# A shorter schedule for the convolution stages of a four-part image kernel: stages one step closer, one signal split in two

## The reference

```python
t = t + dwconv(t, cpe1_w, cpe1_b)                 # depthwise 3x3, "cpe1"
tn = layernorm_over_channels(t)                   # n1_g, n1_b are folded into the weights below
act_res = silu(tn @ actproj_w + actproj_b)
ti = tn @ inproj_w + inproj_b
ti = silu(dwconv(ti, dwc_w, dwc_b))               # depthwise 3x3, "dwc"
ta = attention(ti)                                # keys, queries, a third depthwise conv "lepe"
t = t + (ta * act_res) @ outproj_w + outproj_b
```

## Time and profile before

| | us |
|---|---|
| median of 3 runs | 3499.59 |
| lowest, highest | 3496.89, 3507.64 |
| the profiled execution: its time | 3514.0 |
| its span, first to last instruction | 3512.2 |
| PE busy | 2946.8 (84%) |
| DVE busy | 2289.3 (65%) |
| ACT busy | 2212.2 (63%) |
| POOL busy | 645.5 (18%) |
| mean granted TensorE clock | 0.939 of full |

### The profile page before, as it was taken

The page is one execution under the profiler, slowest core; times in us unless marked ns, Lnnn a source line. Parts: engine busy times, 40 slices in busy tenths (PEclk is TensorE's granted clock), DMA queues, the critical chain, the costliest instruction groups (busy, mean ns, idle before and its releaser), DMA issues. The chain is left out here.

```text
span 3512.2 us, 56298 instructions
## 1 busy us (share of the span) xinstructions
PE 2946.8 (84%) x18996; PEld 1552.5 (44%) x18996; DVE 2289.3 (65%) x2743; ACT 2212.2 (63%) x2537; POOL 645.5 (18%) x420
## 2 busy tenths in 40 slices
PE   3788877979988887798998887787998988788799
PEld 2344335335544433534554443443555444353355
DVE  5677656667468765577655965667756696475772
ACT  2787645557668754546767964554767777464474
POOL 0025200610003510060000540024000153004200
PEclk9999998989999999898999999998999999998899
DMA  2000556700110156570020015854002004476201
GB/s 66 22 1 15 147 144 175 178 14 0 63 37 1 41 125 171 152 173 10 0 81 19 0 55 130 223 142 113 9 14 85 0 0 121 120 200 163 60 0 54
DMA packets 158335, 274.52 MB, mean 78 GB/s; under 512 B 19844, under 2 KB 120903, under 8 KB 158151
## 3 DMA queue, kind: packets, MB, share of 16 engines
q1 hardware_dynamic: 158150, 272.02, 29.0%
HBM read 194.07 MB, written 77.88 MB: 77 GB/s over the span
## 5 line engine op out<-in xcount | busy, mean ns | idle before, releaser
L1007 PE MATMUL psum<-region,m_fc 128*128 (+1 forms) x768 | 294.2, 507 | 19.6 <-DVE region L1655 11.7
L273 DVE SCALAR_TENSOR_TENSOR region<-region,cols 128x768 f32<-128x768 f32 x288 | 292.9, 1017 | 22.8 <-DVE region L273 9.2
L729 POOL TENSOR_TENSOR region<-work,region 128x768 f32<-128x768 f32 x48 | 87.0, 1812 | 1017.6 <-DVE work L1627 1017.6
L1281 PE MATMUL psum<-work,m_fc 128*128 128x384 f32 x768 | 270.6, 486 | 0.0
L700 POOL TENSOR_TENSOR work<-work,region 128x768 f32<-128x768 f32 x96 | 174.5, 1817 | 505.5 <-DVE work L1448 505.5
L960 ACT ACTIVATE work<-psum,cols 128x768 f32<-128x768 f32 x192 | 173.0, 901 | 142.1 <-PE psum L1007 141.6
L1007 PE MATMUL psum<-work,m_avg 128*128 128x384 f32 x576 | 227.4, 519 | 15.1 <-ACT work L836 7.2
L1007 PE MATMUL psum<-region,m_cen 128*128 (+1 forms) x384 | 157.1, 535 | 88.1 <-DVE region L1508 49.9
L1518 DVE SCALAR_TENSOR_TENSOR work<-region,cols,work 128x768 f32<-128x768 f32 x192 | 200.6, 1045 | 11.5 <-DVE work L1518 5.2
L1007 PEld LDWEIGHTS psum<-region,m_fc 128*128 128x128 f32 x768 | 140.9, 195 | 148.3 <-ACT work L960 46.7
L681 POOL MEMSET region<- 128x98 f32 (+1 forms) x20 | 4.2, 209 | 1043.2 <-DVE region L1649 627.2
(11 more groups left out here) (236 smaller groups left out, 6895.3 us busy)
## 6 DMA issues: line engine op xcount, KB each, us to landing
work<-scratch_cpe SPq DMA_DIRECT2D x192, 196.0 KB, 4.0
work<-scratch_dwc SPq DMA_DIRECT2D x192, 196.0 KB, 4.1
work<-scratch_lepe SPq DMA_DIRECT2D x192, 196.0 KB, 3.9
region<-in_tab_ch SPq DMA_DIRECT2D x192, 192.0 KB, 3.8
region<-in_x SPq DMA_DIRECT2D x48, 384.0 KB, 3.3
region<-in_tab_tok SPq DMA_DIRECT2D x48, 384.0 KB, 3.2
out<-work SPq DMA_DIRECT2D x48, 384.0 KB, 2.3
scratch_cpe<-region SPq DMA_DIRECT2D x44, 392.0 KB, 4.3
```

What stands on the lines that cost most here:

```text
L273: eng.scalar_tensor_tensor(out=tgt, in0=prow(k, b, *TAPS[n]), scalar=tap_weight(conv, TAPS[n]), in1=tgt, op0=ALU.mult, op1=ALU.add).then_i ...
L729: g.tensor_tensor(region_tile(3, 4 + p), tile(p), region_tile(3, 2 * p), ALU.mult).then_inc(f2_qc, 1)
L1007: last = pe.matmul(psum[:, bank + s, 0:HC], weights[:, :], moving(s), start=(n == 0), stop=(n == len(terms) - 1))
L1281: last = pe.matmul(psum[:, 4 + s, 0:HC], fc2[:, P * j:P * (j + 1)], static(tile(4 + j))(s), start=(j == 0), stop=(j == 3))
```

## The change

It closes up the schedule and splits a signal:

- `cpe1_run`: the order within a step and the lags. PE was `centre` (lag 3), `var` (4), `convolve` (1) and is `convolve` (1), `var` (3), `centre` (2). ACT was centre tap (0), `squares` (3), `root` (4) and is centre tap (0), `root` (3), `squares` (2). DVE was `normalise` (5), `add_taps` (2), `left`, `right` (1) and is `left`, `right` (1), `normalise` (4), `add_taps` (1).
- `dwc_run`: everything behind the input products is a step closer: the shifted products and taps five blocks behind, not six; the run starts at step 27, not 28, and the keys at 41, not 43.
- `in_act`: the product with `m_w_in` gets a signal of its own, `e2_in`, on which `ti` now waits. It waits only for its own banks. The product with `m_w_act` follows, with the waits that belong to its banks.

```diff
+        e2_in = signal("e2_in", "p")
...
# ScalarE
-                cpe1_run = [(0, cpe1_centre), (3, squares), (4, root)]
+                cpe1_run = [(0, cpe1_centre), (3, root), (2, squares)]
-                dwc_run = [(0, silu_act), (5, dwc_centre), (7, silu_v)]
+                dwc_run = [(0, silu_act), (4, dwc_centre), (6, silu_v)]
-                overlapped(a, NB, [(0, norm_run), (NB + 1, cpe1_run), (2 * NB + 4, dwc_run),
-                                   (3 * NB + 7, [(0, stage), (2, key_exp)])])
+                overlapped(a, NB, [(0, norm_run), (NB + 1, cpe1_run), (2 * NB + 3, dwc_run),
+                                   (3 * NB + 5, [(0, stage), (2, key_exp)])])
...
# TensorE
-                cpe1_run = [(3, centre), (4, var), (1, convolve)]
+                cpe1_run = [(1, convolve), (3, var), (2, centre)]
 
                 def in_act(b, p):
+                    if is_first(b):
+                        pe.wait_ge(e1["t"], done(i, NB - 1))
+                    pe.wait_ge(e2_ti, done(i, b - 1))
+                    product(0, [(w_in, flat_rows(2, b))]).then_inc(e2_in, 1)
                     if isinstance(b, int) and b < 2:
                         pe.wait_ge(e1["tn"], done(i, NB - 2 + b))
-                    pe.wait_ge(e2_ti, done(i, b - 1))
                     pe.wait_ge(e2_act, done(i, b - 1))
-                    product(0, [(w_in, flat_rows(2, b))])
                     product(2, [(w_act, flat_rows(2, b))]).then_inc(e2_mm, 1)
-                dwc_run = [(0, in_act), (6, dwc)]
+                dwc_run = [(0, in_act), (5, dwc)]
-                overlapped(pe, NB, [(0, norm_run), (NB + 1, cpe1_run), (2 * NB + 4, dwc_run),
-                                    (3 * NB + 7, [(4, kv_sum), (1, keys)])])
+                overlapped(pe, NB, [(0, norm_run), (NB + 1, cpe1_run), (2 * NB + 3, dwc_run),
+                                    (3 * NB + 5, [(4, kv_sum), (1, keys)])])
...
# VectorE
-                cpe1_run = [(5, normalise), (2, add_taps), (1, left), (1, right)]
+                cpe1_run = [(1, left), (1, right), (4, normalise), (1, add_taps)]
                 def ti(b, p):
-                    v.wait_ge(e2_mm, done(i, b))
+                    v.wait_ge(e2_in, done(i, b))
-                dwc_run = [(6, left), (6, right), (0, ti), (6, add_taps)]
+                dwc_run = [(5, left), (5, right), (0, ti), (5, add_taps)]
-                overlapped(v, NB, [(0, norm_run), (NB + 1, cpe1_run), (2 * NB + 4, dwc_run),
-                                   (3 * NB + 7, [(3, key_phi), (2, key_in), (3, key_turned)])])
+                overlapped(v, NB, [(0, norm_run), (NB + 1, cpe1_run), (2 * NB + 3, dwc_run),
+                                   (3 * NB + 5, [(3, key_phi), (2, key_in), (3, key_turned)])])
```

## The result

The changed kernel took **3417.8 us** (median of 4 runs, 3414.0 to 3427.1) against 3501.6 for the kernel before in the same comparison: a ratio of 0.9769, 95% interval 0.9744 to 0.9795, 84 us less. The forecast was 3415.6, within 3402 to 3452.

The account below looks back on a forecast made before the run. Stage order, neither PE nor a transfer, sets the `cpe1_run` step. Terms sum to -21.0 us an image, -84 for four: 3430 from the profiled 3514.0, 3415.6 against the median of 3499.6; range 3402 to 3452.

Parts of the forecast that it names:

- start: Start of `cpe1_run`: `add_taps` ahead of `residual` on DVE makes the last product of `norm_run` later; +1.0 us an image.
- steady `cpe1_run`: Nine steps between `convolve` of block 2 and block 11: PE sets a step of 4.87 us; -9.1 us an image.
- allowance for transfers: Steady `cpe1_run`: loads and store just fit the step; +1.0 us an image for single late loads, bounds 0 and 11.4.
- tail: Last `convolve` to first `in_act`: 11.8 us against 16.0, first `m_w_in` product no longer waiting for `normalise`; -4.2 an image.
- fill: First `in_act` to first shifted product: six input products of 2.78 us, 16.7 against 27.4; -10.7 us an image.
- `dwc_run` behind it: From the first shifted product on: transfers count, and moved input products delay one load's issue; +1.0 us an image.
- the ring: In `cpe1_run`, the chain `centre`, `squares`, `var`, root, `normalise`, next `centre`: as long as before, now spanning two steps.
- the 0.8 us spare ahead of `squares`: Steady `cpe1_run` on ACT: `squares` ends at 6.2 us, the next `var` needs it at 7.0, so 0.8 is spare.
- The slower rival: In `cpe1_run` the chain from `centre` to `normalise` closes within every step: 8.7 us a step, 3548 in all; chance 0.04.
- The rival of a step of 5.5: Transfers bound both runs: `cpe1_run` settles at 5.5 us a step, 19 us more over four images, 3434; chance 0.15.
- The estimate from the Trainium skill's 189 GB/s: In `cpe1_run`, a block's loads take 4.2 us; store behind them, step 5.5, gain about 19 us less over four images.
- The split: Division of the shortening between first `in_act` and first shifted product: 7.9 us from the signal, 2.8 from the shorter lag.

Follow-up runs that it names:

- the ACT experiment: Changed kernel with `squares` put ahead of `root` again in ACT's order for `cpe1_run`; 3453.1 us, ratio 0.9865 to the kernel before.
- the second store: Changed kernel with each block of the image stored again to a spare place, loads waiting for both stores; 3424.9 us, ratio 0.9768 to the kernel before.
- the run with four blocks: Changed kernel with shifted products of `dwc_run` four blocks behind, not five, and the keys a step earlier; 3411.6 us, ratio 0.9745 to the kernel before.
- the one with other partitions: Changed kernel with each load's four transfers taking two rows for all 128 partitions, not all rows for 32; 3926.7 us, ratio 1.1206.
- The residual edit: Changed kernel with DVE's `residual` in `norm_run` one step earlier and last in its step; 3403.7 us, ratio 0.9718 to the kernel before.

## Why the prediction was right

Its steps, an image, against the means of the table:

| step | forecast | measured |
|---|---|---|
| start | +1.0 | +1.5 |
| steady `cpe1_run`, with the allowance for transfers | -9.1 + 1.0 | -9.0 |
| tail | -4.2 | -4.3 |
| fill | -10.7 | -11.3 |
| `dwc_run` behind it | +1.0 | +0.9 |
| sum | -21.0 | -22.2 |

*Steady `cpe1_run`.* Right: 4.88 us a step, PE without a gap. That the ring spans two steps is what the ACT experiment takes away: the 0.8 us spare ahead of `squares` was real, and the order on ACT was what kept it. The slower rival had the right mechanism, a ring that closes in each step, but priced it at 8.7; with `squares` first it closed at 5.6, since `convolve` and `var` stay beside it.

*Transfers.* The allowance of 1.0 was not needed: 35 of the 36 steps are 4.88, one is 5.02. The rival of a step of 5.5 is refuted by the changed kernel's 258 GB/s in a step of 4.88, and the second store shows that some 300 can be had. The estimate from the Trainium skill's 189 GB/s (page "SBUF — State Buffer", section "Door 1: The DMA port swizzle") gave the same step and fell with it. But the loads alone are 0.803 MB in 4.88 us, 165 GB/s and under that figure; what failed is the sum that put the store behind them. The one load measured by itself, at 201 GB/s, is a little above the figure.

*Tail.* 11.7 for 11.8. Two gaps of 1.27 us before `var`, at the full clock, as written.

*Fill.* 16.4 for 16.7. Six `in_act` take 2.73 each and not 2.78: PE doesn't wait for `ti`, as forecast, and the product behind `m_w_act` starts mostly 1.29 after it, where the forecast took 1.39 for both. The step before was taken from one image, whose fill was 27.4; the mean was 27.7. The split was forecast at 7.9 for the signal and 2.8 for the lag and measured at 8.7 and 2.7. The loads stayed hidden; the run with four blocks shows how near the end of that was.

*`dwc_run`.* Its size is right; the reason is only in part. The moved `in_act` brings 2.7 us of work into the stretch, and the waits on loads fell by 12.3 / 4 = 3.1: it fills a wait, as said. What makes the stretch longer is something else: 0.3 us of wait on `ti` in the first step, 0.3 on `add_taps` (L1539), and PE's busy time, which rose by 3.3 and not 2.7; the part of it at the lower clock is 6.8 us an image, before 6.0. None of that was in the forecast, and the size is no sharp test of it: single images scatter from 52.3 to 55.4 before and from 54.0 to 56.2 after.

*Start.* This is the term that was mis-sized. I took the wait of `l1_out` on `residual` as later by one DVE instruction, which it was (3.01 to 4.00), and left the clock as it was in the image I read. But that image already ran at the lower clock. In the profiles of the old order (before, and the three runs that keep it) the start took 10.2 us in 11 of 16 images and 13.1 or 13.2 in 5; with the new order it took 12.8 to 13.7 in all 24 images of six runs (leaving out the one with other partitions, which holds up the loads). Against the old order's mean of 11.1 this is +2.0, against an image that kept the clock +3. The granted clock of the stretch tells the two apart in the kernel before: here the last `l1_out` of the third image, to be laid beside that of the second, then the stretch in the second and the third image:

```profile
2103.15 1.53 PE L1007 MATMUL psum<-region,m_w_l1out 128*128 128x384 f32 x4 [3.01 <-DVE region L1493]
```
```profile
1240.34:1253.47 13.13, 10.12 (x106) 3.75 (x105) 10.17 (x12) 2.68 (x4) 4.16 (x9) 0.74 0.39 95
2097.98:2108.20 10.22, 7.21 (x105) 2.93 (x105) 10.10 (x12) 2.68 (x4) 3.90 (x9) 1.00 0.50 123
```

The same idle time of 3.01 us stood in both, and what decided between them stays open. With 4.00 the granted clock of the stretch was 0.75 or 0.87 in each of the 24 images, and 1.00 in none. The residual edit takes 2.3 us of the idle time away and brings 1.00 in that stretch, with 3.7 us an image and 14 in all; the start is where the change had given most back.

*The total.* That the medians differ by 84 us, just as forecast, is partly luck. In the profiled executions the stretches differ by 88.7 us, some 5 more than forecast: 1.7 us an image more came from the allowance that wasn't needed and from tail, fill and `dwc_run`, 0.5 less from the start. That the medians don't show the 5 lies within the scatter outside of the stretches. What the table bears out is the terms, each to within 1 us.

## What to carry to other kernels

If stages of several blocks share a ring of engines, look for what stands ahead of a ready instruction in an engine's queue for no reason but order: a root behind an unrelated square closed the ring in each step and cost more than half of what the order had gained in steps and tail, although ACT was busy for less than two thirds of the step (3.4 us of 5.6). When one result of a pair of products is wanted early, signal it on its own. And read a small shift of a wait on TensorE in all images of a trace, not in one: one microsecond more of idle cost two on average, and three against an image that had kept the clock.

## What the runs showed of the hardware

- A DMA share of 1.00 in the windows is not a full DMA: at the same share this kernel moved 258 GB/s, and 294 to 317 with a store more. It wasn't far from a limit either: those steps were 0.6 us longer on average, with waits on loads.
- Four transfers whose outermost dimension is four ran at some 98 GB/s, with a busy share that fits a quarter of the engines (0.2 to 0.3); a step of `cpe1_run` took 9.1 us on average in place of 4.88, and the whole kernel 15% longer than the changed one (12% longer than the one before), for the same bytes.
- The same idle time ahead of the last `l1_out`, 3.00 to 3.02 us, was followed by a stretch at the full clock of 2.4 GHz in 11 images and by one that began at the lower level of 1.2 GHz in 5 (granted clock 1.00 and 0.74). With 3.99 to 4.01 us it was lower in all 24 (0.75 or 0.87), with 0.3 in none of 8. In the second image of the changed kernel two products of 1.56 and 2.17 us took 2.90 and 3.31.
